# The last output tiles of a four-layer graph network: tile 6 sent from ScalarE's own queue

## The reference

```python
x = _layernorm(x + _L0_gnn_ref(x, edge_index, ...), axis=-1)
x = _layernorm(x + _L1_gnn_ref(x, ..., src, dst, 1024), axis=-1)
x = _layernorm(x + _L2_gnn_ref(x, ..., edge_index), axis=-1)
x = _layernorm(x + _L3_gnn_ref(x, edge_index, ...), axis=-1)   # attention with 8 heads
return x                                                       # (1024, 512) float32
```

## Time and profile before

| what | value |
|---|---|
| device time, median of 3 | 403.72 us (403.42 to 404.16) |
| device time of the profiled execution | 403.67 us |
| its span, first to last instruction | 401.8 us |
| TensorE busy | 370.4 us, 92% of the span |
| VectorE busy | 278.4 us, 69% |
| ScalarE busy | 230.0 us, 57% |
| GpSimd busy | 93.7 us, 23% |
| output transfers | 8 of 256 KB, by SP, 2.5 us in the middle from issue to landing |

### The profile page before, as it was taken

One profiled execution on the slowest core, in us unless ns is written; L12 is line 12 of the kernel. 1 busy time (PEld: TensorE's weight loads), 2 busy tenths in 40 slices (PEclk: granted clock), 3 DMA queues, 4 the chain that ended last, 5 costly groups with the idle time before them and its releaser, 6 DMA issues.

```text
span 401.8 us, 7998 instructions
## 1 busy us (share of the span) xinstructions
PE 370.4 (92%) x2704; PEld 216.0 (54%) x2704; DVE 278.4 (69%) x603; ACT 230.0 (57%) x390; POOL 93.7 (23%) x87
## 2 busy tenths in 40 slices
PE   1799889999999999999999999999798999999990
PEld 1254346444444444444444444444346889999990
DVE  7769998946996677024653222555798688999984
ACT  9789875566822145312562111246444999999444
POOL 4520000019940066500594000133100000012110
PEclk9999999999999999999999999999999999999996
DMA  5950004104100000000243000033202122210005
GB/s 180 390 178 2 1 0 160 52 0 148 64 0 2 1 0 3 2 0 0 42 91 78 0 2 2 2 76 79 54 1 63 46 68 93 97 64 2 4 3 212
DMA packets 27447, 22.71 MB, mean 57 GB/s; under 512 B 19536, under 2 KB 19728, under 8 KB 27408
## 3 DMA queue, kind: packets, MB, share of 16 engines
q1 hardware_dynamic: 26544, 19.06, 15.9%
q10 hardware_dynamic: 864, 3.15, 2.4%
HBM read 15.87 MB, written 2.13 MB: 45 GB/s over the span
## 4 chain that ended last, share of the span: by engine, by line
PE 74%; DVE 14%; issue 5%; ACT 3%; DVEq 2%; ACTq 0%
PE ps L726 15%; PE ps L1084 14%; PE ps L935 7%; PE ps L976 7%; PE ps L889 7%; PE ps L898 7%; PE ps L1025 7%; DVE c L1238 4%; PE ps L879 3%; PE ps L759 3%; PE ps L868 3%; DVE big L1473 2%; DVE adj L1219 1%; PE ps L780 1%; DVEq L1238 1%
## 5 line engine op out<-in xcount | busy, mean ns | idle before, releaser
L726 PE MATMUL ps<-big,xTs 128*128 128x512 f16 x384 | 84.4, 379 | 3.0 <-DVE cts L1460 3.0
L726 PEld LDWEIGHTS ps<-big,xTs 128*128 (+1 forms) x384 | 37.0, 98 | 47.0 <-issue 3.5
L635 ACT ACTIVATE big<-big,uvt 128x1024 bf16<-128x1024 f32 x55 | 59.0, 1153 | 0.0
L425 POOL TENSOR_TENSOR big<-xcur,big x24 | 27.8, 1157 | 119.6 <-ACT xcur L546 119.0
L545 ACT ACTIVATE big<-xcur,nmr,rstd x24 | 19.6, 815 | 38.8 <-DVE nmr L1344 38.8
L759 PE MATMUL ps<-big,xTs 128*128 128x512 f32 x64 | 35.3, 648 | 0.0
L453 ACT ACTIVATE big<-ps 128x512 f16<-128x512 f32 (+2 forms) x17 | 9.8, 574 | 39.9 <-PE ps L726 30.0
L1238 DVE TENSOR_TENSOR c<-c,ps 128x80 f32 (+31 forms) x64 | 23.3, 364 | 9.7 <-PE ps L780 5.6
L395 POOL TENSOR_TENSOR big<-xTs,big 128x2048 f16<-128x2048 f32 x4 | 16.3, 4086 | 58.8 <-ACT big L453 58.8
L1025 PE MATMUL ps<-big,cst 128*128 128x260 f16 x256 | 29.8, 275 | 0.0
L780 PE MATMUL ps<-adj,cts 128*128 128x80 f16 (+31 forms) x128 | 21.3, 271 | 8.9 <-DVE c L1238 4.8
(11 more groups left out here) (206 smaller groups left out, 651.8 us busy)
## 6 DMA issues: line engine op xcount, KB each, us to landing
big<-u_rows ACTq DMA_DIRECT2D x6, 512.0 KB, 3.7
xTs<-in_xT SPq DMA_DIRECT2D x2, 1024.0 KB, 9.4
xcur<-in_x SPq DMA_DIRECT2D x1, 2048.0 KB, 17.8
out<-xcur SPq DMA_DIRECT2D x8, 256.0 KB, 2.5
big<-in_W SPq DMA_DIRECT2D x1, 1024.0 KB, 6.1
cts<-in_W3T SPq DMA_DIRECT2D x1, 1024.0 KB, 13.1
xTs<-in_W1T SPq DMA_DIRECT2D x1, 1024.0 KB, 5.4
xTs<-in_wc SPq DMA_DIRECT2D x1, 1024.0 KB, 8.2
```

The source lines that it names most:

```text
L425: pool.tensor_tensor(cur[:, 1, 1, t, :], xcur[:, t, :], cur[:, 1, 0, t, :], ALU.subtract).then_inc(S["x_lo"], 1)
L635: act.activation(above[:, a % AHEAD, :], uf[:, h % 2], ACT.Relu, scale=BIG, bias=vb[:, j, h:h + 1]).then_inc(S["above_in"], 1)
L726: return mm(bank, lhs(k)[a], rhs(k)[b], start=start and k == 0 and n == 0, stop=stop and k == KT - 1 and n == 2)
```

## The change

Tile 6 leaves SP's loop. ScalarE issues it, after both arms of its `If`, once its seven scalings have raised `out_act` to 7. SP sends tiles 0 to 5 and then 7. The semaphore that counts the landings and SP's last wait for all eight stay as they were.

```diff
 NORM_ACT, NORM_DVE = (0, 1, 2, 3, 4, 5, 6), (7,)
+OUT_ACT = NORM_ACT[-1]
...
-            for t in range(NT):
+            for t in (t for t in range(NT) if t != OUT_ACT):
                 if t in NORM_ACT:
                     sp.wait_ge(S["out_act"], NORM_ACT.index(t) + 1)
...
                 for t in NORM_ACT:
                     act.activation(xcur[:, t, :], xcur[:, t, :], ACT.Identity, bias=nmr[:, t:t + 1], scale=rstd[:, t:t + 1]).then_inc(S["out_act"], 1)
+
+            act.wait_ge(S["out_act"], len(NORM_ACT))
+            act.dma_start(out.rearrange("(t p) d -> t p d", p=P)[OUT_ACT], xcur[:, OUT_ACT, :]).then_inc(S["out_done"], 16)
```

## The result

The changed kernel takes 404.56 us (median of 22 runs, 403.47 to 405.49); the kernel before, run beside it 22 times, takes 403.68 us. The ratio is 1.0023 with a 95% interval of 1.0017 to 1.0029: slower by about 0.9 us, where 403.7 and no change were forecast. The measured time lies 0.3 us above the forecast range of 402.9 to 404.3.

A forecast was written before the change was run, and what follows sets the result against it. The end was taken as bound by two DMA engines with three tiles' backlog plus a 0.69 us fetch each; completion and barrier stay. Profiled 403.67 us less 0.04, put back to the median, gave 403.7, range 402.9 to 404.3.

The forecast's parts named there:

- What bounds the end: After the last scaling: two DMA engines, moving one fetch and their share of three tiles after 397.98, end the kernel.
- The backlog of the DMA engines: Output tiles 5, 6 and 7: 0.70 us each in any order, from 397.98 to 400.09, as before.
- SP's order: SP's last issues: tile 7 issued at 397.53 behind tile 5, 0.70 us earlier, then waiting 0.32 us for busy engines.
- Tile 6 on ScalarE: ScalarE's transfer behind both arms: issued at 397.88, 0.05 us after its scaling, taking 326 to 349 ns like its others.
- the cover: Engines busy with tiles 5 and 7 until 399.39: 0.56 to 0.68 us of slack; issue may start up to 398.5.
- The signs towards slower: At the end: ScalarE's transfer starting later than 0.6 us after its scaling, or ScalarE's drain after SP's release.
- The rival on the jump: ScalarE's jump lacks instructions and takes 3.1 us, so tile 6's issue starts at 400.0; 404.3 to 405.5, chance 0.06.
- The size: Whole kernel: gain of 0.04 us, bounds 0 and 0.08, from idle time within the backlog; 403.7 us.
- The carried-through gain: Rival at the output's end: tile 7's earlier issue lands it 0.70 us earlier, wholly or in part; 403.0, chance 0.20.

The follow-up runs named there:

- e1: Changed kernel with tile 6's transfer moved into both of ScalarE's arms, ahead of its jump; 403.83 us, ratio 1.0007 to the kernel before.
- e9: Kernel before (SP sends all tiles) with the other, never-run arms of ScalarE and VectorE left out; 402.89 us, ratio 0.9978.
- e2: Kernel before with only SP's order changed: SP sends all eight tiles, 7 ahead of 6; ratio 1.0003 to the kernel before.
- e5: Changed kernel with tile 6's scaling also put behind both arms, right ahead of its transfer; 404.25 us, ratio 1.0014 to the kernel before.
- e7: e1 with tile 6's transfer held back by two ScalarE copies on scratch; 404.20 us, ratio 1.0019 to the kernel before.
- e8: e7 with VectorE's other, never-run arm left out as well; ratio 1.0002 to the kernel before.
- e10: e1 with the other, never-run arms of ScalarE and VectorE left out; 402.90 us, ratio 0.9979 to the kernel before.
- e3: Changed kernel with ScalarE's other, never-run arm left out, so ScalarE has no jump over it; 403.92 us, ratio 1.0006 to the kernel before.
- e11: Changed places of the two arms on ScalarE and VectorE, whole algorithm kept, ScalarE sending tile 6; ratio 0.9986 to the kernel before.
- e4: Changed kernel with VectorE's other, never-run arm left out, so VectorE does not jump far; 403.36 us, ratio 0.9996 to the kernel before.

## Why the prediction was wrong

- *What bounds the end* was right for the kernel before. The backlog of the DMA engines and the fetches on two of them set the end: e1, with three tiles in another order on two queues, has the release of before within 0.05 us, and e9 removes the tail.
- *SP's order* was right: 0.37 us between the issues where 0.38 was forecast, no effect on the time that e2's interval shows.
- *Tile 6 on ScalarE* is the step that failed: "Its transfers took 326 to 349 ns to issue", and with it the cover that "would hide a slow issue of this length". The price was taken from six transfers in the middle of the arm, which have no jump ahead of them. Behind the jump the issue took 2.27 us, 1.9 us more, and its end at 2.30 us behind the scaling lies far outside the cover, which ended 0.67 us behind it. The start was right to 0.02 us. The signs towards slower were set on when the transfer starts and on ScalarE's drain, and neither showed; what was long was the issue itself.
- *The rival on the jump* had the place and the sign, at 0.06. It was put down by "the same jump took 0.4 us before, and two more rows behind it move its target nowhere". The 0.4 us hold (0.43 in e5) and do not help, since it is not the jump that is slow but a transfer issued 1.0 to 1.3 us behind it. The measured 404.56 us lie inside this rival's 404.3 to 405.5, by luck: it had the transfer start late, at 400.0, and it started on time. Two fetches stood in the earlier trace rows; I counted what they take from the DMA engines, and did not ask which jumps they belong to and what else they come with.
- *The size*. Tile 6's data ends at about 401.0 on 15 engines. With 0.4 us to land this is 3.9 us behind the scaling, 0.3 more than before. The rest of the profiled 4.91 us is one engine that is 0.9 us late. VectorE's later fetch, which now comes ahead of that engine's share of tile 6, accounts for 0.71 of it; the rest stays open. No term of the prediction had this fetch. In the medians the whole loss is 0.9 us. The split rests on single traces, and on e7 against e8, which changes it by 0.87 us in the release and 0.17% in the ratios.
- *The carried-through gain*, the likeliest rival, had nothing in it: e10 is no faster than e9.

What holds the transfer's issue stays open. The runs show that ScalarE's own jump is needed (e3, e1), that VectorE's makes the hold longer (1.57 against 2.27 us in one trace each), and that ordinary ScalarE instructions are not held (e5, e11). The fetch alone does not cover the time: in the changed kernel the two early fetches are on the DMA engines for 0.31 us each and over by 398.5, 1.2 us or more before the issue ends. In e4 the only one is over by 398.5, 0.9 us or more before. A jump without a fetch was not tried.

## What to carry to other kernels

Put a transfer ahead of the engine's jump, or on an engine that has not just jumped (0.38 us of issue here against 2.27), and take the price of an issue from rows that have the same thing ahead of them. At the end of this kernel an instruction fetch was a load on one DMA engine like any other. Where the DMA engines set the end, try the arm that runs as the last one, so that no engine jumps there: it was worth 0.14% here. A second queue gave nothing where the backlog and not the issue set the landing (402.90 against 402.89 us).

## What was not expected of the hardware

- A transfer issued by ScalarE 1.0 to 1.3 us behind the start of its jump took 1.57 to 2.27 us to issue in four kernels; without a jump 0.37 to 0.38 us in six. An activation behind the same jump started after 0.43 us, and activations 1.9 to 2.7 us behind another jump ran undisturbed (e11).
- Instruction fetches of 0.65 to 0.72 us, each on one DMA engine, delayed the whole output by about that much: SP's release came 0.85 us earlier without them (e9, 2.75 against 3.60 us). Two arms that never run cost the kernel before 0.22% through the jumps over them.
